# Dealing the PSUM banks of a two-block transformer kernel by phase: single banks while both attention passes are causal

## What is computed

```python
x = x + 0.5 * _L0_ffn_ref(_layernorm(x), ...)      # its own attention (16 heads of 8, not causal), then 8 experts, top 1
x = x + _L0_attn_ref(_layernorm(x), ...)           # causal attention
x = x + 0.5 * _L0_ffn_ref(_layernorm(x), ...)
x = x + 0.5 * _L1_ffn_ref(_layernorm(x), ...)      # 128 -> 512 -> 128, two low-rank variants, summed
x = x + _L1_attn_ref(_layernorm(x), ...)           # causal attention
x = x + 0.5 * _L1_ffn_ref(_layernorm(x), ...)
```

## Time and profile before

| | |
|---|---|
| time, median of 3 runs | 1050.1 us (1044.61 to 1054.32) |
| the profiled execution | 1051.72 us |
| its span, first to last instruction | 1049.9 us |
| mean granted TensorE clock | 0.956 of full speed |
| busy: TensorE matmul, VectorE, ScalarE, GpSimd | 908.4, 779.2, 675.5, 340.5 us |
| first and last reduction of a causal p1 (line 896) | 331.2 and 979.9 us from the span's start |

### The profile page before, as it was taken

The page is one execution under the profiler, slowest core; times in us unless marked ns, Lnnn a source line. Parts: engine busy times, 40 slices in busy tenths (PEclk is TensorE's granted clock), DMA queues, the critical chain, the costliest instruction groups (busy, mean ns, idle before and its releaser), DMA issues.

```text
span 1049.9 us, 25343 instructions
## 1 busy us (share of the span) xinstructions
PE 908.4 (87%) x10020; PEld 481.1 (46%) x10020; DVE 779.2 (74%) x1412; ACT 675.5 (64%) x1470; POOL 340.5 (32%) x603
## 2 busy tenths in 40 slices
PE   2799999899577899998999998886898889999997
PEld 1132333227575455554323332275764545555554
DVE  5889999845356887789899998554665688888555
ACT  2388878686364578777888877874543157667631
POOL 4443322333645222422324113436541032311100
PEclk9599999999899899999999999998898989999999
DMA  4117730010222221112110100102111022110000
GB/s 145 41 42 183 182 98 2 14 48 17 79 81 77 57 56 45 42 44 55 30 43 22 43 2 12 50 14 79 43 41 41 21 62 64 33 34 4 3 22 20
DMA packets 60520, 52.29 MB, mean 50 GB/s; under 512 B 9106, under 2 KB 57362, under 8 KB 60402
## 3 DMA queue, kind: packets, MB, share of 16 engines
q1 hardware_dynamic: 48980, 40.00, 14.2%
q10 hardware_dynamic: 8478, 4.62, 2.1%
q0 software_dynamic: 2944, 6.05, 1.8%
HBM read 13.64 MB, written 11.06 MB: 24 GB/s over the span
## 4 chain that ended last, share of the span: by engine, by line
PE 51%; DVE 21%; ACT 11%; issue 10%; POOL 3%; DMA 2%; another core or an unknown queue 1%; ACTq 0%; DVEq 0%; SPq 0%; POOLq 0%
PE ps L544 14%; PE ps L620 12%; DVE negm L905 8%; ACT pt L738 8%; DVE blockm L896 4%; PE ps L683 3%; PE ps L575 3%; PE ps L669 3%; PE ps L675 3%; PE ps L689 3%; PE ps L550 2%; PE ps L580 1%; PE ps L628 1%; PE ps L638 1%; DVE a_stats L849 1%
## 5 line engine op out<-in xcount | busy, mean ns | idle before, releaser
L738 ACT ACTIVATE pt<-ps 128x512 f32<-128x512 f32 (+1 forms) x896 | 457.5, 566 | 163.6 <-PE ps L544 115.0
L905 DVE TENSOR_REDUCE negm<-ps 128x2 f32<-128x1024 f32 x256 | 300.4, 1218 | 34.4 <-PE ps L544 31.3
L620 PE MATMUL ps<-pt,va 128*32 128x256 f32 (+1 forms) x4352 | 275.3, 342 | 13.4 <-ACT ot L744 5.5
L896 DVE TENSOR_REDUCE blockm<-ps 128x8 f32<-128x1024 f32 (+1 forms) x192 | 195.4, 1042 | 41.5 <-PE ps L544 27.2
L544 PE MATMUL ps<-ks,qs 61*128 61x128 bf16 (+2 forms) x1536 | 174.4, 294 | 37.3 <-DVE negm L905 16.2
L544 PE MATMUL ps<-qs,ks 64*128 64x128 bf16 (+3 forms) x1408 | 169.2, 297 | 9.8 <-ACT parts L720 3.0
L620 PEld LDWEIGHTS ps<-pt,va 128*32 128x32 f32 x4352 | 92.5, 109 | 124.9 <-issue 81.2
L544 PEld LDWEIGHTS ps<-ks,qs 61*128 61x128 bf16 x1536 | 54.8, 95 | 192.7 <-issue 88.7
L1174 POOL CAST mpart<-negm 128x16 bf16<-128x16 f32 x64 | 13.2, 206 | 291.9 <-DVE negm L905 126.1
L772 ACT ACTIVATE stage<-ps,pt 128x128 f32<-128x128 f32 x240 | 68.6, 371 | 48.5 <-PE ps L669 33.7
L544 PEld LDWEIGHTS ps<-qs,ks 64*128 64x128 bf16 x1408 | 58.1, 95 | 65.8 <-ACT pt L738 44.1
(11 more groups left out here) (151 smaller groups left out, 1026.2 us busy)
## 6 DMA issues: line engine op xcount, KB each, us to landing
qs<-parts SPq DMA_DIRECT2D x80, 128.0 KB
ks<-parts SPq DMA_DIRECT2D x77, 128.0 KB
experts<-in_experts SPq DMA_DIRECT2D x8, 578.0 KB, 5.4
sorted<-stage ACTq DMA_DIRECT2D x4, 967.5 KB, 8.3
qs<-mrow SPq DMA_DIRECT2D x128, 6.0 KB
pt<-y_rows SPq DMA_DIRECT2D x8, 256.0 KB, 3.2
qs<-parts SPq DMA_DIRECT2D x32, 56.0 KB
ks<-parts SPq DMA_DIRECT2D x30, 56.0 KB
```

The costliest lines, as they stand in the source:

```text
L620: ins = pe.matmul(pv_bank[32 * j:32 * j + 32, q0:q1], va[n % 2][:, kb, value_at(g, j):value_at(g, j) + 32], pt[:, k_, from_:from_ + q1 - q ...
L738: a.activation(pt[:, k_ % NPT, S * s:S * s + width], b_bank(o + s)[:, 0:width], ACT.Exp).then_inc(b_free, 1)
L896: v.tensor_reduce(blockm[:, g % 2, :, t, PLACES[c_]], pair_of(ka)[:, :, 0:width].rearrange("p s (b c) -> p s b c", c=P), AX, ALU.max, nega ...
L905: v.tensor_reduce(negm[:, g % 2, :, t, c_], pair_of(ka), AX, ALU.max, negate=True).then_inc(a_free, 1)
```

## The change

The rings now depend on the phase. While the latest p1 and the latest p2 in the event list are both of causal batches ("narrow"), A jobs take turns on three single banks 0, 1, 2 and B jobs on four single banks 3, 4, 5, 6. A causal p1 in that phase takes two A turns, one for each of its two heads, with a count of a_full after each, and VectorE reads it with two reductions of half the size, each of which frees its bank. Otherwise the pairs (0, 1), (2, 3) and the banks 4, 5, 6 serve as before, also for a causal p1 whose p2 counterpart is still of a batch that is not causal. In the list, 166 of the 192 causal p1 and 180 of the 192 causal p2 fall in a narrow phase; there are two such phases, from the first p2 of batch 4 to the first p1 of batch 8, and from the first p2 of batch 12 to the end. Instead of a fixed distance, TensorE's wait before a job is for the last users of the banks that it takes (before[ev]), in either ring.

```diff
+BANKS_A = [[(0, 1), (2, 3)], [(0,), (1,), (2,)]]
+BANKS_B = [[(4,), (5,), (6,)], [(3,), (4,), (5,), (6,)]]
...
+        def take(ev, ring, banks):
+
+            jobs_ = banks_a if ring == "a" else banks_b
+            before.setdefault(ev, []).extend(user[b] for b in banks if b in user)
+            jobs_.append(banks)
+            for b in banks:
+                user[b] = (ring, len(jobs_))
+
+        def next_of(ring, choices):
+            t = turn.get((ring, len(choices)), 0)
+            turn[(ring, len(choices))] = t + 1
+            return choices[t % len(choices)]
+
+        causal_now = dict(p1=False, p2=False)
         for ev in plan:
             name = ev[0]
+            if name in causal_now:
+                causal_now[name] = causal_of[ev[1]]
+            narrow = all(causal_now.values())
             if name in A_JOBS:
-                at_a[ev] = ordinal["a"]
-                ordinal["a"] += 1
+                at_a[ev] = len(banks_a)
+                if name == "p1" and narrow:
+                    single.add(ev)
+                for _ in range(2 if ev in single else 1):
+                    take(ev, "a", next_of("a", BANKS_A[narrow]))
             if name in B_JOBS:
-                at_b[ev] = ordinal["b"]
-                ordinal["b"] += 2 if name == "p2" else 1
+                at_b[ev] = len(banks_b)
+                for _ in range(2 if name == "p2" else 1):
+                    take(ev, "b", next_of("b", BANKS_B[narrow]))
...
                 if name in A_JOBS:
                     ka = at_a[ev]
-                    need(pe, a_free, ka - 1)
                 if name in B_JOBS:
                     o = at_b[ev]
-                    need(pe, b_free, o - 1 if name == "p2" else o - 2)
+                for ring, done in before.get(ev, ()):
+                    need(pe, a_free if ring == "a" else b_free, done)
...
+                    if ev in single:
+                        ends[0].then_inc(a_full, 1)
                     ends[1].then_inc(a_full, 1)
...
-                        v.tensor_reduce(blockm[:, g % 2, :, t, PLACES[c_]],
-                                        pair_of(ka)[:, :, 0:width].rearrange("p s (b c) -> p s b c", c=P), AX, ALU.max,
-                                        negate=True).then_inc(a_free, 1)
+                        for s in range(2 if ev in single else 1):
+                            heads = slice(s, s + 1) if ev in single else slice(0, 2)
+                            banks = ps[:, banks_a[ka + s][0], :].rearrange("p (s c) -> p s c", s=1) if ev in single \
+                                else pair_of(ka)
+                            need(v, a_full, ka + s + 1)
+                            v.tensor_reduce(blockm[:, g % 2, heads, t, PLACES[c_]],
+                                            banks[:, :, 0:width].rearrange("p s (b c) -> p s b c", c=P), AX, ALU.max,
+                                            negate=True).then_inc(a_free, 1)
```

More of the change, by code:

```diff
@@ L254, in program @@
         pv_bank = ps[:, 7, :]
-        first_b = 4
-        nbanks_b = 3
         NT = TB * NB
@@ L428, in program @@
         at_a, at_b, at_step, at_pv, at_m, at_evac, at_quad, pv_of_step = {}, {}, {}, {}, {}, {}, {}, {}
-        ordinal = dict(a=0, b=0)
+        banks_a, banks_b, before = [], [], {}
+        user = {}
+        turn = {}
+        single = set()
         ATTENTION = ("stats", "rstd", "norm", "keep", "hT", "q", "k", "v", "qrem", "krem", "qmid", "kmid", "qlo", "klo",
@@ L475, in pair_of @@
         def pair_of(k):
-            return ps[:, 2 * (k % 2):2 * (k % 2) + 2, :]
+            return ps[:, banks_a[k][0]:banks_a[k][0] + 2, :]
         def a_tiles(k):
-            return ps[:, 2 * (k % 2), :].rearrange("p (i c) -> p i c", c=P)
+            return ps[:, banks_a[k][0], :].rearrange("p (i c) -> p i c", c=P)
         def b_bank(o):
-            return ps[:, first_b + o % nbanks_b, :]
+            return ps[:, banks_b[o][0], :]
         def b_tiles(o):
@@ L588, in pe_program @@
                     ends = score_pieces(pe, PASS1[w["causal"]][c_], w["causal"] and c_ == 0,
-                                        [pair_of(ka)[:, s, :] for s in range(2)],
+                                        [ps[:, banks_a[ka + s][0], :] if ev in single else pair_of(ka)[:, s, :]
+                                         for s in range(2)],
                                         [qs[n % NQK][rows[s], 2 * g + t, :] for s in range(2)],
                                         [ks[n % NQK][rows[s], 2 * g + t, :] for s in range(2)], mask_q)
+                    if ev in single:
+                        ends[0].then_inc(a_full, 1)
                     ends[1].then_inc(a_full, 1)
@@ L895, in dve_program @@
                         width = max(col + k1 - k0 for _, col, k0, k1 in PASS1[True][c_])
-                        v.tensor_reduce(blockm[:, g % 2, :, t, PLACES[c_]],
-                                        pair_of(ka)[:, :, 0:width].rearrange("p s (b c) -> p s b c", c=P), AX, ALU.max,
-                                        negate=True).then_inc(a_free, 1)
+                        for s in range(2 if ev in single else 1):
[6 more added lines that the diff above has]
+                                            negate=True).then_inc(a_free, 1)
                         if ev == final_p1(n, g):
-                            need(v, a_free, ka + 1)
+                            need(v, a_free, ka + (2 if ev in single else 1))
                             v.tensor_reduce(negm[:, g % 2].rearrange("p s t i -> p (s t i)"),
@@ L1275, in stack @@
             if n >= NQK:
-                need(eng, a_full, at_a[final_p1(n - NQK, 3)] + 1)
+                need(eng, a_full, at_a[final_p1(n - NQK, 3)] + (2 if final_p1(n - NQK, 3) in single else 1))
                 need(eng, b_full, at_b[final_p2(n - NQK, 3)] + 2)
```

## The result

The changed kernel took 1056.5 us (median) where the kernel before took 1047.6 in the same runs: a ratio of 1.0089, 95% interval 1.0071 to 1.0108. It is 0.9% slower. The time lies inside the range and within the 1% that the forecast called no change, but the sum said +0.35 us and the runs say +8.9.

The account below looks back on a forecast made before the run. No engine alone was taken as the bound; TensorE, VectorE and ScalarE hand it to each other. Gains of 5.2 us and costs of 1.4, 2.4 and 1.75 sum to +0.35, forecast 1051 us, range 1038 to 1069.

Parts of the forecast that it names:

- the sum: Whole kernel: -5.2 + 1.4 + 2.4 + 1.75 = 0.35 us, as good as nothing.
- Nothing: Non-causal phases, changes of rings and the dense tail: put at no effect; a ring change's one wait under 1.2 us.
- B ring: p2 on four banks in narrow phases: waits shrink, about 0.7 us gained a batch, 5.2 us in all.
- The share of 0.1 for evac: The two quads with an evac: 0.1 us gained for one later p2, nothing more.
- The rival in which pv takes the wait's place: At pv: it waits for the same exponentials anyway, so 5.2 us are not gained; some 1057 us, chance 0.14.
- Loop of the A ring: p1 on three single banks: loop of 1.40 us against kind 0's 1.34 us slot, costing 0.2 a batch, 1.4 us.
- VectorE the bound: Narrow p1 of kinds 0 and 1: each split stands on the path, 13 to 26 us; 1068 us, chance 0.25.
- Less slack: A jobs where VectorE has other work: 0.4 us in each of six statistics quads (2.4), plus 1.75 at guard and norm.
- VectorE's spare time: In narrow phases it hides the 166 splits' 8 to 26 us of VectorE work, where it is spare.
- At 941.85: Second stage, p1 while VectorE is at the NaN guard: 1.0 us late, 1.1 us staying up to o.
- The place at 914.22: Second stage, where VectorE also has guard and next layer norm: 0.65 us lost by the same sum.
- Stalls go: Both causal stages: four banks remove all TensorE idle time, 13.5 us; 1038 us, chance 0.18.

Follow-up runs that it names:

- e9: The changed kernel with one wait per ring before a job instead of one for each bank's last user; 1.0032 of the kernel before.
- e5: The changed kernel, but each job takes the bank or pair whose last user is the oldest, not the next by turn; 1.0074 of the kernel before.
- e4: The kernel before with all 192 causal reductions split in two, banks and waits unchanged; 1.0038 of the kernel before.
- e8: The changed kernel with narrow dealing in batches 12 to 15 alone, batches 4 to 7 dealt as before; 1.0115 of the kernel before.
- e2: The changed kernel without the fourth B bank: three single A banks, three B banks; 1.0148 of the kernel before.
- e3: The changed kernel with the fourth B bank given to the A ring: four single A banks, three B banks; 1.0054 of the kernel before.
- e10: The kernel before with a second wait, always already over, added before each p2; 1.0096 of the kernel before.
- e12: The changed kernel with one wait per ring, oldest bank first, narrow dealing only up to the second quad of batch 14; 0.9986 of the kernel before.

## Why the prediction came out as it did

**The step that failed** is the paragraph "Nothing", and in it two sentences: "Phases that are not causal keep banks and waits" and "The change of rings costs one wait each, under a reduction's 1.2 us." The first was taken from the banks alone. The waits changed in every phase, because the diff replaces one count by one count for each bank. The price of that is 8.9 - 3.2 = 5.7 us between the changed kernel and e9, known to some 2.6 us by the two intervals. The quads and batches bear it out: the second waits add 37.91 - 37.44 = 0.47 us to a causal batch under narrow dealing and 45.82 - 45.60 = 0.22 to one that is not causal, by 6.9 and 8 batches 3.2 and 1.8 us.

The second sentence missed the turn of the new ring. The quads after the two first p2 took 1.85 and 0.76 us longer, and 1.60 and 0.65 of it went when the oldest bank was dealt (e5).

**B ring.** Forecast 0.7 us a batch, 0.63 of it in the plain quad and the one with q and k; measured 0.82, with 0.92 in those two. The share of 0.1 for evac was wrong in sign (8.74 with four banks, 8.64 with three). The rival in which pv takes the wait's place falls by the same number.

**Loop of the A ring.** Forecast 1.40 us, measured 1.40 without the second wait. It is a little over the slot, as the prediction had it. The rival "VectorE the bound" got its sign of slots at 1.4 us or more, but neither its period of 39 us (37.90) nor its chain with more than 30% VectorE (22 and 25% from 345 to 480 and from 850 to 980 us).

**Less slack.** The quad with statistics was given 0.4 and lost 0.46 in e9, 0.67 with the second waits. The prediction put it all on the shorter ring; e4 shows 0.27 of it to be the split, which the prediction had left to VectorE's spare time. In the last quads with guard and norm the price was 1.75 us, from two places. At 941.85 it was 1.1, and the two quads over which that stretch reaches are 0.63 and 0.48 us longer in e9 than before: right. The place at 914.22, with 0.65, lies in the first quad of batch 14, which is 0.69 us shorter in e9. But there the clock differs. The windows of this quad, first the kernel before, then e9, the changed kernel and e8 (columns as above):

```profile
907.35:919.03 11.68, 9.73 (x157) 5.27 (x153) 9.96 (x23) 7.17 (x17) 4.34 (x8) 0.85 0.25 67
906.16:917.15 10.99, 8.42 (x165) 4.95 (x161) 10.36 (x28) 7.18 (x16) 4.33 (x8) 1.00 0.28 72
909.94:921.12 11.18, 8.46 (x165) 5.23 (x161) 10.35 (x28) 7.19 (x16) 4.34 (x8) 1.00 0.27 72
908.69:921.16 12.47, 9.82 (x165) 6.01 (x161) 10.53 (x28) 7.25 (x16) 4.35 (x8) 0.86 0.26 67
```

In the kernel before the granted clock was 0.50 (1.2 of 2.4 GHz) from 915.6 to 919.0 us, after TensorE had idled 1.87 us for VectorE; in e9 it was 1.00 throughout. e8 and the changed kernel deal this stage alike, and there such a stretch costs 12.47 - 11.18 = 1.29 us. At full clock the kernel before would so take some 10.4 us here, an estimate from these rows, and e9's 10.99 is then a loss of 0.6, near the forecast 0.65. The next quad is 0.58 shorter, of which 0.23 is what every plain quad gained; it is the 8.05 of the kernel before that stands out from its other plain quads' 7.70. A third quad, the last, is 0.63 longer, for which there was no term. The quad with evac lost 0.25 that no term had either; e2 and e3 put 0.21 on the third A bank.

**The sum.** For a steady batch the terms say -0.7 + 0.2 + 0.4 = -0.1 us, and e9 has 37.44 - 37.53 = -0.09. That this agrees so well is partly luck: the quad with q and k gained 0.57 us where its terms say 0.3, and the one with evac and o lost 0.25 where they say about nothing. Still, most prices read from the trace had the right place and size, and the forecast would have been nearer without the two that were put at nothing. "Stalls go" fell: no version's period came near 36 us.

**What stays open.** e9's quads account for 1.6 of its 3.2 us (some 2.9 if the 1.3 of batch 14's first quad are set right), e4's, which has the same low stretch of the clock there as the kernel before, for 2.0 of 4.2, and e10's, with the 1.9 outside, for 6.7 of 10.2. The mean granted TensorE clock over the timed runs was lower than that of the kernel before in every edited kernel, by 0.0005 (e3, no more than the scatter of the runs) to 0.0065 (e10); in e9 it was 0.9529 for 0.9571, in e12 0.9558 for 0.9580. In the kernel before, the time is about 0.6 us longer for each 0.001 of clock that is missing, from run to run, so this is of the size of the rest. It does not explain e9's gain on the changed kernel, whose runs had 0.9540, more than e9's. Why the mean clock should depend on these edits, no run here shows.

## What to carry to other kernels

When a diff rewrites how a wait is computed, count the waits in every phase, not only where the resource changes: two counts of one semaphore can be two instructions, while one wait for the later count does the same. Compare edits by a row that repeats once per unit of work; where it repeats within 0.02 us, it finds a price of 0.1 us that the whole time shows only as an unexplained rest. Look at the granted clock of such a row's stretch before its length is put down to the edit. When two deals of a resource meet, look at the last user of the first unit that the new deal hands out.

## What the runs showed of the hardware

A second wait instruction ahead of a matmul makes its weight load start some 0.06 us later after the release that it waits for (0.46 for 0.40 on p2, 1.46 to 1.48 for 1.40 in the loop of p1), although the first of the two counts had long been reached. Over the loads from 345 to 480 us whose idle time before is over the floor, the median time from the release to the load is 0.043 us on p2 of the kernel before and 0.105 in e10, 0.043 on p1 of e9 and 0.104 in the changed kernel. Where no second wait instruction stands, as in the slots of kind 0 of e10's plain quad, which take 1.35 us as before, nothing is lost. Whether one costs nothing where the release is early, no run here shows.
